# A Fourier tower and token layers on one core: halved relus and by-pair transforms, an early fetch of the tokens, 64-row tiles for the token products

## The reference, cut to what matters

```python
def tower(x, ...):                       # x (32, 64, 64, 1)
    v = concat([x, gx, gy]) @ p_w + p_b  # 32 channels
    for i in range(4):
        x1 = irfft2(modes of rfft2(v) times W1, W2)   # 12 x 12 modes at two corners
        x2 = einsum("bcxy,cd->bdxy", v, w_w[i]) + w_b[i]
        v = batchnorm(x1 + x2)
        if i < 3: v = relu(v)
    return einsum("bcxy,cu->bxyu", v, q_w) + q_b      # (32, 64, 64): 32 x 64 tokens of 64
...
def attn(x, ...):                        # 4 layers, 8 heads of 8
    for i in range(4):
        h = layernorm(x)
        q, k, v = softmax(h @ Wq * s, -1), softmax(h @ Wk * s, tokens), h @ Wv
        x = x + (q @ (k^T v)) @ Wo + bo               # per image and head
        h = layernorm(x)
        x = x + gelu(h @ W1 + b1) @ W2 + b2
    return x
...
# then a mixture of four experts, two chosen per token, with a shared one, and a last layernorm
```

## Time and profile before

| | us |
|---|---|
| median of 3 runs | 772.47 |
| lowest and highest | 770.98, 776.26 |
| the profiled execution, in all | 773.5 |
| its span, first to last instruction | 771.7 |
| busy: TensorE, VectorE, ScalarE, GpSimd | 626.0, 546.1, 362.3, 71.1 |
| granted TensorE clock, mean | 0.907 |

### The profile page before, as it was taken

The page is one execution under the profiler, slowest core; times in us unless marked ns, Lnnn a source line. Parts: engine busy times, 40 slices in busy tenths (PEclk is TensorE's granted clock), DMA queues, the critical chain, the costliest instruction groups (busy, mean ns, idle before and its releaser), DMA issues. The chain is left out here.

```text
span 771.7 us, 25833 instructions
## 1 busy us (share of the span) xinstructions
PE 626.0 (81%) x11935; PEld 434.3 (56%) x11935; DVE 546.1 (71%) x810; ACT 362.3 (47%) x517; POOL 71.1 (9%) x126
## 2 busy tenths in 40 slices
PE   5989974766899955766999937888776999999997
PEld 3967751323877742334877723332532888777754
DVE  4568887994567878994488889987741768667363
ACT  0034459600035459500044565737221688888763
POOL 3100000002100000003000000002000223233200
PEclk9599997998599987998699969999978999999999
DMA  9200000005100000006000000013003300000001
GB/s 348 101 3 3 4 23 1 1 2 200 50 3 3 3 2 1 2 1 247 4 3 3 3 8 2 2 42 137 6 8 95 112 2 2 1 3 2 2 0 29
DMA packets 13925, 28.15 MB, mean 36 GB/s; under 512 B 5613, under 2 KB 6125, under 8 KB 13689
## 3 DMA queue, kind: packets, MB, share of 16 engines
q1 hardware_dynamic: 13528, 25.77, 9.5%
q10 hardware_dynamic: 288, 0.73, 0.3%
HBM read 25.44 MB, written 1.05 MB: 34 GB/s over the span
## 5 line engine op out<-in xcount | busy, mean ns | idle before, releaser
L461 ACT ACTIVATE V<-ps,wts 128x1024 f32<-128x1024 f32 x96 | 101.8, 1111 | 260.3 <-PE ps L926 260.3
L592 DVE BATCH_NORM_STATS2 stats<-V 128x6 f32<-128x512 f32 x192 | 117.7, 677 | 24.5 <-ACT V L461 24.5
L926 PE MATMUL ps<-tab,A 64*128 64x128 f32 x1536 | 105.2, 283 | 13.6 <-ACT V L461 7.8
L926 PEld LDWEIGHTS ps<-tab,A 64*128 64x128 f32 x1536 | 91.9, 189 | 37.3 <-issue 22.2
L534 DVE STREAM_TRANSPOSE A<-V 128x2048 f32<-128x2048 f32 x48 | 107.4, 2278 | 6.2 <-ACT V L440 6.2
L801 PE MATMUL ps<-A,tab 128*128 128x384 f32 x192 | 75.1, 539 | 32.7 <-DVE A L541 32.7
L440 ACT ACTIVATE V<-V,small 128x2048 f32<-128x2048 f32 x48 | 96.2, 2084 | 3.8 <-DVE small L639 3.8
L789 PE MATMUL ps<-A,tab 32*32 32x512 f32 x1536 | 60.5, 648 | 35.4 <-DVE A L534 35.4
L801 PEld LDWEIGHTS ps<-A,tab 128*128 128x128 f32 x192 | 37.4, 204 | 79.1 <-DVE A L541 59.8
L583 DVE STREAM_TRANSPOSE A<-ps 128x2048 f32<-128x2048 f32 (+1 forms) x27 | 55.4, 2071 | 25.9 <-PE ps L913 25.9
L541 DVE STREAM_TRANSPOSE A<-ps 128x1024 f32<-128x1024 f32 x48 | 56.6, 1219 | 10.9 <-PE ps L789 10.9
(11 more groups left out here) (257 smaller groups left out, 857.3 us busy)
## 6 DMA issues: line engine op xcount, KB each, us to landing
A<-in_modes SPq DMA_DIRECT2D x32, 384.0 KB, 7.1
r_ky<-in_modes SPq DMA_DIRECT2D x16, 384.0 KB, 5.6
wl<-in_layers SPq DMA_DIRECT2D x3, 452.0 KB, 5.4
V<-in_pixels SPq DMA_DIRECT2D x1, 1024.0 KB, 12.8
wm<-in_mixture SPq DMA_DIRECT2D x1, 874.5 KB, 7.7
tab<-in_table SPq DMA_DIRECT2D x1, 656.5 KB
A<-in_turned SPq DMA_DIRECT2D x1, 512.0 KB
tower_out<-A SPq DMA_DIRECT2D x4, 128.0 KB, 2.3
```

Source lines behind the costliest of these rows:

```text
L461: nc.scalar.activation(Vm[:, 2 * h:2 * h + 2, r, 512 * q:512 * (q + 1)], bank(half_of_u(q, r) + 2 * h, 2).rearrange("p (m n) -> p m n", m= ...
L592: last = nc.vector.bn_stats(stats[:, 16 * q + 4 * r + m, :], Vm[:, m, r, 512 * q:512 * (q + 1)])
L926: last = nc.tensor.matmul(ps[:, at:at + P], G[(2 * q + quad) % 4][rows, x:x + P], inv_y[rows, :], start=step < 2 and quad == 0, stop=step ...
```

## The change

It has three parts.

1. *Forward transform.* For pairs 0 and 1 the relu and the turn are each made in two halves of 1024 columns, with a semaphore for the first half. The first and the last `forward_y` of a layer become `forward_y_by_pairs`: all 32 matmuls for one pair over 256 columns, then the 32 for the other, with one signal at the end. So such a step has 64 matmuls instead of 32.
2. *Hand-over.* `r_ky` outlives the tower; `u0` lies in it, and so do two tables, `turn` (an identity) and `in_order`, which SP loads before the second store. SP reads group 0 back after it has issued store 1 and store 0 has landed, group 1 likewise after store 2. The tower no longer waits for its last store. The token block reads group 2 and group 3, each once its own store has landed. TensorE waits for the first tokens and tables instead of `cst`, and for `cst` before it centres. Some semaphores of the tower are merged (`s_step`), with the same order of work.
3. *Token products.* The weights per layer shrink from 904 to 648 columns, as the zeros are gone. k and the output product become two matmuls in 64x64 tiles, one per parity. q and v come from one load: h, 64 rows by 128 tokens, is loaded and 128 columns of weights (q and v) pass, two tiles side by side; their halves land in two banks. There is one signal for k, q and v of a group. The first feed-forward product uses four 64x64 tiles, 8 matmuls a group for 4. v is copied inside ScalarE's loop of exponentials; the transposes of ke now wait for it, and the turned queries go into k's place.

The diff, cut to its core:

```diff
...
+def token_rows(tower_out, q, b2):
+    return tower_out.rearrange("a (r q t b y) -> b q (a r) t y", r=4, q=4, b=2, y=S)[b2, q]
+def token_room(room, q, b2):
+    at = N_TURN + 256 * q
+    return room[S * b2:S * (b2 + 1), at:at + 256].rearrange("p (t y) -> p t y", y=S)
...
-            sp.dma_start(late, table[:, T_LATE:T_DRAM]).then_inc(s_late, 16)
+            sp.dma_start(late, table[:, T_LATE:T_TURN]).then_inc(s_late, 16)
             for q in range(OCT):
+                if q == 1:
+                    sp.wait_ge(s_step, 1)
+                    sp.dma_start(r_ky[:, 0:N_TURN], table[:, T_TURN:T_DRAM]).then_inc(s_tokens[0], 16)
                 sp.wait_ge(s_ua, 2 * (q + 1))
                 sp.wait_ge(s_uv, 2 * (q + 1))
                 sp.dma_start(tower_out.rearrange("a (r n) -> a r n", r=4)[:, :, 512 * q:512 * (q + 1)],
-                             A[0:P:8, 2048 * q:2048 * (q + 1)].rearrange("p (r n) -> p r n", r=4)).then_inc(s_out, 16)
-            sp.wait_ge(s_out, 16 * OCT)
+                             A[0:P:8, 2048 * q:2048 * (q + 1)].rearrange("p (r n) -> p r n", r=4)).then_inc(s_out[q], 16)
+                if q in (1, 2):
+                    sp.wait_ge(s_out[q - 1], 16)
+                    for b2 in range(2):
+                        sp.dma_start(token_room(r_ky, q - 1, b2), token_rows(tower_out, q - 1, b2)).then_inc(s_tokens[q - 1], 16)
...
-                pair = Vk[:, :, P * n:P * (n + 1)]
-                nc.scalar.activation(pair, pair, ACT.Relu, bias=bias, scale=scale).then_inc(s_relu, 1)
+                for k in range(0, 16, 8 if n < 2 else 16):
+                    pair = Vk[:, k:k + 8 if n < 2 else 16, P * n:P * (n + 1)]
+                    nc.scalar.activation(pair, pair, ACT.Relu, bias=bias, scale=scale).then_inc(s_relu_half if n < 2 and k == 0 else s_relu, 1)
...
+                    if n < 2:
+                        dve.wait_ge(s_relu_half, 2 * (l - 1) + n + 1)
+                        nc.vector.transpose(T[n % 3].rearrange("p (k n) -> p k n", k=16)[:, 0:8], Vk[:, 0:8, P * n:P * (n + 1)])
                     dve.wait_ge(s_relu, PAIRS * (l - 1) + n + 1)
                     if n >= 3:
                         dve.wait_ge(s_fy, FU * (l - 1) + (n - 3) // 2 + 1)
-                    nc.vector.transpose(T[n % 3].rearrange("p (k n) -> p k n", k=16), Vk[:, :, P * n:P * (n + 1)]).then_inc(s_T, 1)
+                    rest = 8 if n < 2 else 0
+                    nc.vector.transpose(T[n % 3].rearrange("p (k n) -> p k n", k=16)[:, rest:], Vk[:, rest:, P * n:P * (n + 1)]).then_inc(s_T, 1)
...
+                def forward_y_by_pairs(u):
+                    at_least(pe, s_Y, PAIRS * (l - 1) + 2 * u)
+                    for p in range(2):
+                        pe.wait_ge(s_T, PAIRS * (l - 1) + 2 * u + p + 1)
+                        slot, place = (2 * u + p) % 3, 1 - p if u % 3 == 1 else p
+                        for yh in range(2):
+                            for j in range(4):
+                                for i in range(4):
+                                    rows = slice(Q * i, Q * (i + 1))
+                                    out = bank(i)[Q * j:Q * (j + 1), 256 * place:256 * (place + 1)]
+                                    last = nc.tensor.matmul(out.rearrange("p (k c) -> p k c", k=8), fwd_y[rows, Q * yh:Q * (yh + 1)],
+                                                            T3[rows, j // 2, yh, slot, 8 * (j % 2):8 * (j % 2) + 8, :],
+                                                            start=yh == 0, stop=yh == 1, tile_position=(Q * i, Q * j))
+                    last.then_inc(s_fy, 1)
...
-                    forward_y(0)
+                    forward_y_by_pairs(0)
                     for u in range(FU):
                         forward_x(u, 0)
                         forward_x(u, 1)
-                        if u + 1 < FU:
+                        if u + 2 < FU:
                             forward_y(u + 1)
+                        elif u + 1 < FU:
+                            forward_y_by_pairs(u + 1)
...
+        turn, in_order, u0 = room[:, 0:P], room[:, P:2 * P], room[:, N_TURN:N_TURN + NX]
...
+        def queries_values(g, i):
+            return bank(g, 0, 0, 1024).rearrange("p (a n) -> p a n", a=2)[:, :, GW + P * i:GW + P * (i + 1)]
...
-            for g in range(G):
+            for g in (2, 3):
+                sp.wait_ge(s_stored[g], 16)
                 for b2 in range(2):
-                    rows = tower_out.rearrange("a (r q t b y) -> b q (a r) t y", r=4, q=GROUPS, b=2, y=S)[b2, g]
-                    sp.dma_start(part(u0, g)[S * b2:S * (b2 + 1), :].rearrange("p (t y) -> p t y", y=S), rows).then_inc(s_u[g], 16)
...
-                for g in range(G):
-                    nc.scalar.copy(part(vs, g), bank(g, 1, GW)).then_inc(s_vs, 1)
+                    nc.scalar.copy(part(vs, g).rearrange("p (t a f) -> p a t f", a=2, f=EMB),
+                                   queries_values(g, 1).rearrange("p a (t f) -> p a t f", f=EMB)).then_inc(s_vs, 1)
...
+                for at, n in ((W_O, 1), (W_2, 2)):
+                    w = wl[:, l, at:at + EMB * n].rearrange("p (a e) -> p a e", e=EMB)
...
-                    dve.wait_ge(s_q, l * G + g + 1)
+                    dve.wait_ge(s_qkv, l * G + g + 1)
                     hmax, kmin = hst[:, 0, GH * g:GH * (g + 1)], kst[:, 0, GT * g:GT * (g + 1)]
-                    q3 = bank(g, 0, GW).rearrange("p (h d) -> p h d", d=DH)
-                    link(nc.vector.reduce_max(hmax, q3, X_AXIS))
-                    nc.vector.tensor_tensor(part(qs, g).rearrange("p (h d) -> p h d", d=DH), q3,
-                                            hmax.unsqueeze(2).broadcast_to([P, GH, DH]), ALU.subtract).then_inc(s_qs, 1)
-                    dve.wait_ge(s_kv, l * G + g + 1)
+                    q4 = queries_values(g, 0).rearrange("p a (h d) -> p a h d", d=DH)
+                    most = hmax.rearrange("p (a h) -> p a h", a=2)
+                    link(nc.vector.reduce_max(most, q4, X_AXIS))
+                    nc.vector.tensor_tensor(part(qs, g).rearrange("p (a h d) -> p a h d", a=2, d=DH), q4,
+                                            most.unsqueeze(3).broadcast_to([P, 2, GP * HEADS, DH]), ALU.subtract).then_inc(s_qs, 1)
...
+            pe.wait_ge(s_u[0], 48)
             for g in range(G):
                 for t in range(GP):
-                    nc.tensor.matmul(bank(g, 0, P * t, P), part(spec, g)[:, P * t:P * (t + 1)], ident, start=t == 0, stop=False)
-                pe.wait_ge(s_u[g], 32)
+                    nc.tensor.matmul(bank(g, 0, P * t, P), part(spec, g)[:, P * t:P * (t + 1)], turn, start=t == 0, stop=False)
+                if g:
+                    pe.wait_ge(s_u[g], 32)
                 for t in range(GP):
                     last = nc.tensor.matmul(bank(g, 0, P * t, P), part(u0, g)[:, P * t:P * (t + 1)], in_order, start=False, stop=t == GP - 1)
                 last.then_inc(s_utr, 1)
+            pe.wait_ge(s_cst, 16)
...
+                    pe.wait_ge(s_wk, l + 1)
+                    for par in range(2):
+                        rows = slice(EMB * par, EMB * (par + 1))
+                        nc.tensor.matmul(bank(g, 1)[rows, :], w[rows, W_K:W_K + EMB], h[rows, :], start=True, stop=True,
+                                         tile_position=(EMB * par, EMB * par))
                     for t in range(GP):
-                        last = nc.tensor.matmul(bank(g, 0, GW)[:, P * t:P * (t + 1)], h[:, P * t:P * (t + 1)],
-                                                w[:, W_QV:W_QV + P], start=True, stop=True)
-                    last.then_inc(s_q, 1)
-                    pe.wait_ge(s_wk, l + 1)
-                    nc.tensor.matmul(bank(g, 1), w[:, W_K:W_K + P], h, start=True, stop=True)
-                    for t in range(GP):
-                        last = nc.tensor.matmul(bank(g, 1, GW)[:, P * t:P * (t + 1)], h[:, P * t:P * (t + 1)],
-                                                w[:, W_QV + P:W_QV + 2 * P], start=True, stop=True)
-                    last.then_inc(s_kv, 1)
+                        for par in range(2):
+                            rows = slice(EMB * par, EMB * (par + 1))
+                            dst = bank(g, par, GW).rearrange("p (w t f) -> p t w f", w=2, f=EMB)[:, t]
+                            last = nc.tensor.matmul(dst, h[rows, P * t:P * (t + 1)],
+                                                    w[rows, W_QV:W_QV + P].rearrange("p (w f) -> p w f", w=2),
+                                                    start=True, stop=True, tile_position=(EMB * par, 0))
+                    last.then_inc(s_qkv, 1)
                 for g in range(G):
                     pe.wait_ge(s_ke, l * G + g + 1)
                     pe.wait_ge(s_qs, l * G + g + 1)
+                    pe.wait_ge(s_vs, l * G + g + 1)
...
-                        last = nc.tensor.transpose(bank(g, 0, GW + P * t, P), part(qs, g)[:, P * t:P * (t + 1)], ident)
```

(16 more changed lines are left out.)

92 lines of the change are left out of this document (43 added, 49 removed).

## The result

| | before | after |
|---|---|---|
| median of 20 runs each, us | 772.59 | 766.63 |
| lowest and highest | 766.49, 776.26 | 761.86, 773.78 |
| the profiled execution, in all | 773.5 | 766.84 |
| its span | 771.7 | 765.0 |
| granted TensorE clock, mean | 0.907 | 0.911 |

The ratio is 0.9938, with a 95% interval of 0.9914 to 0.9961: 4.8 us faster by it (3.0 to 6.6), 6.0 by the medians. I had said 761.2, range 757.0 to 766.5, and faster by over 1%. The kernel is faster, but by about half of what I said; the median lies just above my range, and the gain is under 1%.

What follows compares the result with a forecast made beforehand. No single bound was taken: each changed place, with its own limit, got its own sum. Tower 5.8 us plus hand-over 5.5, small terms counted as 0, made 11.3 off 772.5: 761.2, range 757 to 766.5.

Steps and rivals of the forecast that it cites:

- Restart of the forward stage: Start of each forward transform: VectorE goes on 2.3 us earlier in layers 1 and 2, 1.95 in layer 3, 6.6 together.
- The last step by pairs: End of the forward transform: last forward_y by pairs loses 0.1 or 0.66 us a layer, taken as 0.8 over three.
- The condition that I set: Sign of error: the forecast is wrong if the forward stage's end moves less than its start.
- Hand-over: Tower to tokens: early fetch starts centring 6.8 us earlier, 1.5 returned to a low clock; 5.5 won, bounds 3.5 to 7.5.
- hand-over stays cold: Rival at the hand-over: clock does not return before the variance, 3.5 us won instead of 5.5, 763.2; chance 0.15.
- q, k and v: Token layers' product loop: a group takes 0.96 us for 1.32, VectorE's pace is 1.12; 0.1 won a layer, none in layer 0.
- the first rival: Token products: changes of tile drain TensorE, two of 0.24 us a group, about 1.1 a layer, 765.6; chance 0.15.
- The copy of v and the wait of the transposes: Attention: kqT copies come later but the output product has room, so 0; without that room 0.6 us lost a layer.
- Output product and first feed-forward product: Token layers: output product unchanged; first feed-forward product 1.0 us a group for 0.93, 0.3 lost over four layers.
- The serial rival: First feed-forward product: 64x64 tiles sharing rows run one after another, 37 us lost in all, about 798; chance 0.03.
- Token layers as a whole: Sign of error: the forecast is wrong if the token layers change by more than 0.5 us each.
- A clock that falls more often: Rival in the tower: more clock falls in the steady part cost 4.5 us over three layers, 765.7; chance 0.1.

Runs made afterwards that it cites:

- e_hand: Kernel before with the early fetch of the hand-over alone; 772.30 us, ratio 0.9995 to the kernel before.
- e_tok: Kernel before with the new token products in 64-row tiles alone; 778.39 us, ratio 1.0078 to the kernel before.
- e_after: The changed kernel profiled and measured once more, no line different; 768.99 us, ratio 0.9939 to the kernel before.
- e_fwd: Kernel before with the forward transform part alone; 766.93 us, ratio 0.9938 to the kernel before.
- e_fh: Kernel before with forward part and early fetch, old token products kept; 766.97 us, ratio 0.9944 to the kernel before.
- e_order: Changed kernel with group 0's turned queries ahead of group 3's k transposes in TensorE's queue; 764.15 us, ratio 0.9908 to the kernel before.
- e_busy: Changed kernel with the k transposes of groups 1 and 2 made four times over; 764.79 us, ratio 0.9929 to the kernel before.
- e_kfirst: Changed kernel with k of all four groups first, then q and v of all four; 776.74 us, ratio 1.0080 to the kernel before.
- e_warm: Changed kernel with eleven useless TensorE products in the hand-over; 765.90 us, ratio 0.9946 to the kernel before.
- e_best: Changed kernel with eleven useless hand-over products, fourfold k transposes of groups 1 and 2, and group 0's turned queries moved ahead; 762.20 us, ratio 0.9905 to the kernel before.

## Why the prediction was wrong, step by step

**Restart of the forward stage: right, a little too high.** The sum had 2.3, 2.3 and 1.95 us. The starts show 1.98, 1.94 and 1.63, 5.6 for 6.6: both pairs together took 4.09 us, wait included, at a granted clock of 0.61, which is under 2.3 each, but turn 2 starts 6.65 us after the relu and not 6.3, and VectorE's next step hangs on it. **The last step by pairs: sign wrong, size nothing.** In layer 3 the way from the turn of pair 15 to the last first-half result took 4.57 us and not 4.82; I had a loss of 0.1 to 0.66. Over the stage the profiles show 3.3, 3.3 and 1.3 us, because the kernel before happened to have two falls of the clock in each of the first two stages. From the first relu's start to the start of VectorE's last transpose of the stage, the mean of nine stages with the old start (before, e_hand, e_tok) is 67.7 us, of twelve with the new (after, e_after, e_fwd, e_fh) 66.0: 1.7 each, 5.1 in all, and e_fwd's 4.8 agrees. The term was 5.8. In three of the twelve (two of e_after, one of e_fwd) the clock did not come back for the restart but some 11 us later, at 134 to 135 for 123 to 124 in layer 1; they took 66.8, the others 65.5 to 66.3. The sum had no such case. The condition that I set, the end moving less than the start, was met in layer 3 (1.3 for 1.64), by 0.3.

**Hand-over: the first step that failed.** I had 5.5 with a lower bound of 3.5; the profile shows 2.6, the mean over seven kernels with the early fetch and no edit in the hand-over (e_hand, after, e_after, e_fh, e_order, e_busy, e_kfirst) is 14.5 for 17.6 (mean of before, e_fwd, e_tok), 3.0. The term was 6.8 for a warm engine, less 1.5 for a fall of the clock in the wait for group 2, and both are off.

The warm gain is 5.5, not 6.8: e_warm and e_best, with no low clock in the hand-over, take 12.34 for 17.87. The token block starts 1.20 us after the last store's issue, where I had 0.9; the reads of group 2 land 5.5 us after the first issue, where I had 5.2; and three turns, 1.44 us (585.85 to 587.29 in e_best), stand between that landing and the centring, where I had 0.8.

The clock took 2.9 and not 1.5. It fell before the wait: TensorE had 2.13 us without work ahead of 579.84, and within 581 to 582 the granted clock goes to half. So most of the turning, the wait and the centring lie in a low stretch of 10 us. The three turns take 2.71 us for 1.44, and from the centring to the variance it is 3.32 us (588.07 to 591.39) for 1.73. That is the rival "hand-over stays cold", to which I had given 0.15; the earlier trace rows had shown exactly this stretch as cold before the change, and I took a shorter wait as the end of it. In e_after and e_busy the fall came in the wait, as the sum had it, lasted 3.4 us, and cost what I had priced: 13.84 and 13.59 are 1.5 and 1.25 over 12.34. e_order, with a fall that was over before the reads landed, needs 12.26.

**q, k and v: the second.** I had a group at 0.96 us, VectorE setting the pace at 1.12 and 0.1 us won a layer. It is 1.22, VectorE still follows TensorE, and the clean layer loses 0.36. The terms by e_kfirst: two changes of form 0.25 at least where I had nothing, which leaves the products 0.97 at most for 0.96. That is the first rival, which had two of 0.24, 0.48 a group and 1.1 us a layer; the mechanism is there at about half its price a group, and a third of its price a layer. The Trainium skill (TensorEngine Tiling (Array Packing), section Key Properties) says that changing the tiling mode drains TensorE; the runs agree in so far as a change between these forms costs time, 0.125 us or more. The row that I set against it, line 943 in the earlier trace rows, has a change only at either end of 64 entries, and its pace of 23 ns an entry could not have shown 0.1 us.

**The copy of v and the wait of the transposes: 0, for the right reason.** The `kqT` copies came 0.8 us later in the layer, as worked out, and the way to `cx` had the room; e_order took 0.6 of it away and the layer did not move. I had looked for the room on GpSimd's side; the rows show VectorE without a gap up to `cx`. What I did not ask is what the waits do to TensorE: it is busy 2.0 of 4 us there in place of 2.9.

**Output product and first feed-forward product.** The first is as forecast, 1.94 for 1.97. For the second I counted 0.3 lost, and it took 3.68 for 3.72: nothing. The serial rival is out at 58 ns an entry.

**Token layers as a whole: the third.** I wrote that I would be wrong if they changed by more than 0.5 us each. They lost 5.1 us together: 1.3 at the clean stages' lengths (19.40 against 19.18 and three of 19.04), 3.4 in the three stages with a fall (1.27, 1.13 and 1.03 over 19.40), and 0.4 in the feed-forward part of layer 0. A clock that falls more often was one of my rivals, but I had looked for it in the tower. So the forecast of 11.3 became 6.7 in the profiled executions by three terms: the tower gave 9.2, 3.4 more than its 5.8 (of which 2.1 in the forward stages, where the old kernel's clock had fallen more often in that execution); the hand-over gave 2.6, 2.9 less than 5.5; the token layers took 5.1 and not nothing. 11.3 + 3.4 - 2.9 - 5.1 is 6.7.

**What stays open.** Which token stage has a fall is not settled. Thin TensorE work goes with it (e_kfirst, all four; e_hand and e_fh, each in layers 0 and 1, right behind the early start), but the same stretch of the changed kernel goes once with a fall and once without, and in e_best one came behind a busy stretch. So it is not shown either why the parts don't add up, beyond the half microsecond of the smaller weight load.

## What to carry to other kernels

When a wait is shortened, look up the granted clock in the stretch behind it, and let the sum go by that until something is shown to hold the clock up; here a gain of 5.5 us on a warm engine was 2.6 on a cold one. When products are packed tighter, what you win in TensorE's busy time is won in nothing if the next consumer waits for the first result: work out when the first group's last input is ready, not the pace alone. And before pricing a queue, look for the engine that has no gap on the way (here VectorE, from its first step on q to `cx`); what is moved beside it costs nothing until its room is used up.

## What the runs showed of the hardware

- Work without use can pay within a stage: the three kernels with the eleven useless products have no low clock in the hand-over, which takes 12.34, 12.34 and 13.01 us; the seven with the early fetch and without them all have 3.4 to 10.2 us of it and take 12.26 to 15.65. That the kernel as a whole gains by it is not shown (e_warm: 0.9946).
- A change between 64x64 and 64x128 tiles cost 0.125 us or more (e_kfirst). Twelve more transposes of 128x128 a layer cost it nothing: 19.40 in e_busy and in the changed kernel.
- TensorE's busy time can go down and the stage up: with its work drawn together in e_kfirst, the q, k and v products of a layer took 0.75 us less and the stage 2.5 to 3.0 us more, with later queries and 6.8 us at half clock in each.
- The reads of the tokens (64 KB each) landed later beside a bigger load: 5.96 to 6.16 us after the first issue beside weights of 452 KB, 5.31 to 5.64 beside 324 KB (four and seven kernels).
- One and the same kernel gave attention stages of 19.40 and 20.5 us in one execution, with the same instructions; a single profile can't tell such a loss from the edit's.
